# One scan and one product for both channel halves in the selective scan of a hybrid network

## The reference

```python
dt = softplus(dt_lo @ dt_proj_w.T + dt_proj_b)
A = -exp(A_log)
def step(h, inp):
    dt_t, B_t, C_t, x_t = inp
    dA = exp(dt_t[..., None] * A[None])
    h = dA * h + dt_t[..., None] * B_t[:, None, :] * x_t[..., None]
    return h, sum(h * C_t[:, None, :], axis=-1)
_, ys = lax.scan(step, h0, (dt, Bp, Cp, xc))
y = (moveaxis(ys, 0, 1) + Dp * xc) * silu(z)
return einsum('bti,di->btd', y, out_proj_w)
```

## Time and profile before

| what | value |
|---|---|
| median of three runs | 5252.44 us |
| the profiled execution | 5253.41 us |
| its span in the trace | 5251.6 us |
| mean granted TensorE clock | 0.91 |
| share of the span, PE / DVE / ACT / POOL | 80% / 65% / 54% / 38% |
| first and last scan instruction | 1345.4 us and 2366.6 us |

### The profile page before, as it was taken

The page is one execution under the profiler, slowest core; times in us unless marked ns, Lnnn a source line. Parts: engine busy times, 40 slices in busy tenths (PEclk is TensorE's granted clock), DMA queues, the critical chain, the costliest instruction groups (busy, mean ns, idle before and its releaser), DMA issues. The chain is left out here.

```text
span 5251.6 us, 108370 instructions
## 1 busy us (share of the span) xinstructions
PE 4205.7 (80%) x31331; PEld 2104.6 (40%) x31332; DVE 3399.0 (65%) x8427; ACT 2852.9 (54%) x5677; POOL 1970.2 (38%) x2539
## 2 busy tenths in 40 slices
PE   6499999899576766779868888886987788878698
PEld 3144444452222222226312222225973333333597
DVE  3488888448799899894478777762116766665212
ACT  7255555666555555557747676672324455555232
POOL 3000000011677777770403433344536144444452
PEclk9699999999899899899979899897999888888799
DMA  7522222005100000000532222224656332332466
GB/s 259 140 74 73 73 73 74 23 0 197 65 26 26 26 26 26 26 26 0 203 90 81 70 77 72 70 62 133 212 173 224 92 84 79 83 84 62 143 213 191
DMA packets 530984, 489.50 MB, mean 93 GB/s; under 512 B 160546, under 2 KB 468067, under 8 KB 530560
## 3 DMA queue, kind: packets, MB, share of 16 engines
q1 hardware_dynamic: 512496, 448.21, 28.7%
q0 software_dynamic: 18160, 37.42, 2.0%
HBM read 324.32 MB, written 161.09 MB: 92 GB/s over the span
## 5 line engine op out<-in xcount | busy, mean ns | idle before, releaser
L1539 ACT ACTIVATE p_probs<-p_t_ps 128x512 f32<-128x512 f32 (+1 forms) x2304 | 1142.9, 551 | 778.4 <-PE p_t_ps L1353 230.8
L2122 PE MATMUL p_y_ps<-p_prod,c_ident 128*128 128x512 f32 x1024 | 555.8, 669 | 304.1 <-DVE p_prod L2307 299.2
L1366 PE MATMUL p_o_ps<-p_probs,p_v_st 128*32 128x256 f32 (+3 forms) x8704 | 775.8, 432 | 7.4 <-ACT p_o_sb L1525 7.0
L1335 PE MATMUL p_t_ps<-p_t_q,p_t_k 50*128 50x512 bf16 (+3 forms) x3072 | 540.9, 351 | 263.1 <-ACT p_probs L1539 154.8
L1603 DVE TENSOR_REDUCE p_row_max<-p_s_ps 128x1 f32<-128x512 f32 x1024 | 644.8, 681 | 150.4 <-PE p_s_ps L1304 116.0
L2256 POOL TENSOR_TENSOR p_dbx<-p_dtx,p_b_sb 128x512 f32<-128x512 f32 x512 | 632.8, 1272 | 120.6 <-ACT p_b_sb L2153 120.6
L2298 DVE TENSOR_TENSOR_SCAN p_state<-p_da,p_dbx 128x512 f32<-128x512 f32 x512 | 599.2, 1207 | 94.5 <-ACT p_da L2191 76.9
L1241 POOL TENSOR_TENSOR p_v_st<-p_v_raw,p_ones 128x128 f32<-128x128 f32 x192 | 87.5, 456 | 1414.1 <-PE p_o_ps L1366 1358.7
L1304 PE MATMUL p_s_ps<-p_s_k,p_s_q 48*128 48x512 bf16 (+3 forms) x3072 | 508.8, 356 | 122.6 <-DVE p_row_max L1600 49.1
L1600 DVE CUSTOM_DVE_ANT_0 p_tried<-p_s_ps,c_mask_row 128x512 bf16<-128x512 f32 (+3 forms) x1024 | 450.0, 486 | 218.1 <-PE p_s_ps L1304 159.6
L1600 DVE CUSTOM_DVE_ANT_0 p_tried<-p_s_ps,p_s_bias 128x512 bf16<-128x512 f32 (+3 forms) x1024 | 449.6, 485 | 133.8 <-PE p_s_ps L1304 131.3
(11 more groups left out here) (295 smaller groups left out, 7084.9 us busy)
## 6 DMA issues: line engine op xcount, KB each, us to landing
p_wb<-in_w SPq DMA_DIRECT2D x142, 512.0 KB
p_s_q<-stack_q SPq DMA_DIRECT2D x384, 96.0 KB
p_s_k<-stack_k SPq DMA_DIRECT2D x384, 96.0 KB
p_t_q<-stack_q SPq DMA_DIRECT2D x384, 96.0 KB
p_t_k<-stack_k SPq DMA_DIRECT2D x384, 96.0 KB
mamba_inputs<-p_out SPq DMA_DIRECT2D x17, 1536.0 KB, 5.7
p_inp<-mamba_inputs SPq DMA_DIRECT2D x17, 1536.0 KB
p_raw<-routed_rows SPq DMA_DIRECT2D x142, 130.0 KB
```

The costliest lines, as they stand in the source:

```text
L1335: mm = pe.matmul(out[r], t_k[rows, g % 2, pair, c * P:(c + 1) * P], t_q[rows, g % 2, pair, first:first + width], start=True, stop=not mask ...
L1366: mm = pe.matmul(o_ps[32 * j:32 * j + 32, at:to], v_st[:, g % 2, c, j, :], probs[:, g % 2, j, place[c] + at - first:place[c] + to - first] ...
L1539: act.activation(exps, tile, ACT.Exp, scale=scale).then_inc(expd, 1)
L2122: pe.matmul(y_ps[:, h], w["ident"], prod[:, k_slot(n, h, RS)], start=(n == 0), stop=(n == STATE - 1)).then_inc(acc_mm, 1)
```

## The change

Both halves lie side by side in slots of 2T = 1024 columns. One scan instruction runs over both; so that the second half starts at zero, the decay at column 512 is held at zero (set once, and ScalarE writes only 511 columns of the second half). One product with C reads the same 512 columns of C twice. The ring `dbx` has four slots of two halves (the same room), `state` and `prod` double and stay. The decay slots now take four PSUM banks, so C has one bank in place of two and the outgoing product uses B's bank. On VectorE the product of state n-1 stands behind the scan of state n, the gate in state 1. On ScalarE the decay of a state stands ahead of the copy of B, which goes two states ahead. GpSimd waits for a whole scan before it reuses a slot.

```diff
-    R = 8
+    R = 4
+    RP = 2
-    COPIED = 3
+    COPIED = 2
+    OUT_AT = 4
...
-        da = ph.ps("da", [P, RA, T])
-        b_ps, c_ps = ph.ps("b_ps", [P, T]), ph.ps("c_ps", [P, 2, T])
-        y_ps, out_ps = ph.ps("y_ps", [P, 2, T]), ph.ps("out_ps", [P, T])
+        da = ph.ps("da", [P, RA, 2 * T])
+        b_ps, c_ps = ph.ps("b_ps", [P, T]), ph.ps("c_ps", [P, T])
+        y_ps = ph.ps("y_ps", [P, 2, T])
+        out_ps = b_ps
...
-                pe.wait_ge(prod_ready, RS - 4 + 2 * (STATE * b + n) + 2)
-                pe.matmul(c_ps[:, n % 2], w["select"][:, STATE + n], bc[:, u], start=True, stop=True
+                pe.wait_ge(prod_ready, RS + STATE * b + n)
+                pe.matmul(c_ps[:, :], w["select"][:, STATE + n], bc[:, u], start=True, stop=True
...
+                pe.wait_ge(b_ready, 1 + (STATE * (b + 1) + OUT_AT + AHEAD + 1 if follows else STATE * (b + 1)))
...
+                    shared = n == OUT_AT + 1 and not first
+                    if not shared:
+                        next_b(b, u, n, last)
...
+                    sums(b, n, first)
+                    if shared:
+                        pe.wait_ge(added, b + 1)
+                        next_b(b, u, n, last)
...
+                    act.wait_ge(scanned, R + m - RA + 1)
+                    for h in range(2):
+                        if n == 0:
+                            act.wait_ge(dt_ready, 2 + 2 * b + h + 1)
+                        act.activation(da[:, n % RA, h * T + h:h * T + T], dt[:, u, h, h:T], ACT.Exp,
+                                       scale=rate[:, h, n:n + 1]).then_inc(da_ready, 1)
                     if n + COPIED < STATE:
                         copy_b(b, n + COPIED)
...
+                    pool.wait_ge(b_ready, 1 + m + 1)
+                    pool.wait_ge(scanned, m + 1)
...
+            dve.memset(da[:, :, T:T + 1], 0.0).then_inc(rate_ready, 1)
...
+                dve.tensor_tensor_scan(out=state[:, n % RS], data0=da[:, n % RA], data1=dbx[:, n % R], initial=0.0,
                                        op0=ALU.mult, op1=ALU.add).then_inc(scanned, 1)
...
+                dve.wait_ge(acc_mm, 2 * m + 2)
+                dve.tensor_tensor(prod[:, n % RP].rearrange("p (h t) -> p h t", h=2),
+                                  state[:, n % RS].rearrange("p (h t) -> p h t", h=2),
+                                  c_ps[:, :].unsqueeze(1).to_broadcast([P, 2, T]), ALU.mult).then_inc(prod_ready, 1)
...
-                    scan(b, n, 0)
-                    scan(b, n, 1)
-                    if n == 0 and not first:
+                    scan(b, n)
+                    if n:
+                        times_c(b, n - 1)
+                    elif not first:
+                        times_c(b - 1, STATE - 1)
+                    if n == 1 and not first:
                         gate(b - 1, 1 - u)
-                    times_c(b, n, 0)
-                    times_c(b, n, 1)
-                    if n == 6 and not first:
+                    if n == OUT_AT + 2 and not first:
                         add(b - 1)
```

More of the change, by code:

```diff
@@ L2052, in mamba_scan, with half @@
         block = ph.block()
-        def k_slot(n, h, ring=R):
-            return (2 * n + h) % ring
+        def half(h):
+            return slice(h * T, h * T + T)
         @block.sync
@@ L2105, in outward, with sums, next_b @@
                 mm.then_inc(out_mm, 1)
+            def sums(b, n, first):
+                m = STATE * b + n
+                pe.wait_ge(prod_ready, RS + m + 1)
+                for h in range(2):
+                    if n == 0 and not first:
+                        pe.wait_ge(gated_ready, 2 * b + h + 1)
+                    pe.matmul(y_ps[:, h], w["ident"], prod[:, n % RP, half(h)], start=(n == 0), stop=(n == STATE - 1)
+                              ).then_inc(acc_mm, 1)
+            def next_b(b, u, n, last):
+                if n + AHEAD < STATE:
+                    broadcast_b(b, u, n + AHEAD)
+                elif not last:
+                    broadcast_b(b + 1, 1 - u, n + AHEAD - STATE)
             def sequence(b, u, first=False, last=False):
                 for n in range(STATE):
[L2109 to L2112, removed]
+                    shared = n == OUT_AT + 1 and not first
+                    if not shared:
+                        next_b(b, u, n, last)
                     if n + 1 < STATE:
@@ L2126, in sequence @@
                         pe.matmul(y_ps[:, h], skip_w[:, h], inp[:, u, h], start=False, stop=False)
-                    if n == 4 and not first:
+                    if n == OUT_AT and not first:
                         outward(b - 1)
@@ L2141, in _ @@
             sequence(NB - 1, 1, last=True)
-            outward(NB - 1)
+            outward(NB - 1, follows=False)
         @block.scalar
@@ L2185, in sequence @@
                         copy_b(b + 1, n + COPIED - STATE)
[L2186 to L2192, removed]
                     if last:
@@ L2249, in sequence @@
                     m = STATE * b + n
+                    pool.wait_ge(b_ready, 1 + m + 1)
+                    pool.wait_ge(scanned, m + 1)
                     for h in range(2):
-                        k = 2 * m + h
-                        pool.wait_ge(b_ready, 1 + m + 1)
                         if n == 0:
                             pool.wait_ge(dtx_ready, 2 * b + h + 1)
-                        pool.wait_ge(scanned, k + 1)
-                        pool.tensor_tensor(dbx[:, k_slot(n, h)], dtx[:, u, h], b_sb[:, n % RB], ALU.mult
+                        pool.tensor_tensor(dbx[:, n % R, half(h)], dtx[:, u, h], b_sb[:, n % RB], ALU.mult
                                            ).then_inc(dbx_ready, 1)
```

43 lines of the change are left out of this document (16 added, 27 removed).

## The result

The changed kernel takes 5179.8 us in the median of four runs (5174.51 to 5186.83), the kernel before on the same chip 5251.77 (5236.01 to 5255.83). The ratio is 0.9869 [0.9846, 0.9893]: 1.3% faster, 72 us. The forecast was 40 us, so the direction was right and the gain was nearly twice as large.

The account below looks back on a forecast made before the run. VectorE was taken to set the pace, at 64.6 us a sequence. Per sequence 6.9 us gone and 3.9 added, taken as 2.8 less, gave 39 us over 14, with 1 more 40: 5212 against the median, range 5182 to 5243.

Parts of the forecast that it names:

- Merging: VectorE's paired scans and products become one each: 0.14 us saved a state, 3.43 to 3.29, 36 us over 256 states.
- R4: Rival: the merge does not pay, as two banks or repeated columns slow VectorE; 36 us back, 5248; chance 0.07.
- R3: Rival: each removed instruction's fixed part falls out whole, 83 ns more for each of 512, 5170; chance 0.03.
- The three waits: New VectorE waits per sequence: 0.85 before the addition, 1.5 before state 8's scan, 1.6 before the last scan.
- Dp and state 6: Old VectorE waits behind two Dp matmuls and the outgoing product go: 1.3 and 1.5 us a sequence.
- The loop's return: Every second sequence VectorE's own 2.13 us stays; most of the 1.18 behind it is covered, 0.5 a sequence gained.
- The clock: TensorE stretches at 1.2 GHz cost VectorE 1.0 us a sequence instead of about 2.4, so 1.4 gained.
- The spare time: Decays of state n+4 ready at 5.8 us, their scan due at 7.7: 1.7 us to spare on the chain.
- R2: Rival: less is lost, state 8's wait does not come or the clock costs nothing; 21 us, 5191; chance 0.12.
- the wait in state 8: VectorE waits 1.5 us before state 8's scan: late copy of B, two softplus parts, then the decays on ScalarE.
- R1: Rival: the chains are no looser at 1.2 GHz than before; 20 us come back, 5233; chance 0.22.
- R5: Rival: slower, new idle stretches lower TensorE's clock; at half the stage 78 us, 5290; chance 0.05.

Follow-up runs that it names:

- experiment 2: Changed kernel with its one scan and one product per state written as two each, one per half: 5017.95 us, 0.9909 of the kernel before.
- experiment 5: Changed kernel with step size in state 12 (0.9853), outgoing product behind state 8 (0.9829), both plus later addition (0.9788), then GpSimd's correction spread too (0.979).
- experiment 4: Changed kernel, VectorE's loop only: first run waits for its last product before the return, 4998.95 us (0.987); last run covers four sequences a turn, 4995.28 us (0.9878).
- experiment 1: Kernel before with only the new order; halves, two C banks and the outgoing product's own bank stay: 4971.92 us against 5066.54, 0.9814.
- experiment 3: Kernel before with the loop over sequences written out on VectorE alone: 5039.03 us, 0.9948; on GpSimd alone: 5059.17 us, 0.9997.

## Why the prediction came out too small

- **Merging.** Forecast 3.29 us a state, measured 3.31. The price by start-to-start distances was right: 0.12 saved instead of 0.14 (31 us instead of 36, experiment 2). Neither two banks nor repeated columns slow VectorE down (R4): 2283 and 1196 ns are less than twice 1207 and 669. And the fixed part does not fall out whole (R3): the 157 ns for a pair by the Trainium skill's formula (VectorE: DVE Perf Modes, The TRN2 errata) would be 80 us for all 512 instructions, and the runs give 31.
- **The three waits.** Forecast 0.85, 1.5 and 1.6; measured 0.72, 1.22 and 1.52, each in its place and with its releaser. Their causes hold: in experiment 5 the step size and the outgoing product were moved, and the 1.52 and the 1.22 went; the 0.72 went only with the later addition, which brought 1.41 elsewhere. Together they cost 0.5 us a sequence less than I counted (3.7 with their lost overlaps, for 4.2).
- **Dp and state 6.** Both gone, as forecast.
- **The loop's return: the first failed step.** I wrote that VectorE's own 2.13 stays and counted it at every second sequence, 1.05 each. It is 0. I took it for a fixed price of the return. It is a delay from the last issue, and what counts is how much work is queued in front of it. The new order queues a scan and a product (3.31 us) there, and the shorter body makes the delay itself smaller. Either alone takes most of it: with the long body 0.14 and 0.39 are left at the two returns of the last run of experiment 4, with nothing queued 0.8 in its first. I also counted it too often: the loop of six turns jumps back five times, not at each of seven pairs of sequences.
- **The clock: the second failed step.** "With 1.7 to spare I take 1.0; the ends are 0 and the old 2.4." It is 0: every sequence has the same 59.73 us, those with sums at 1.2 GHz too. Two things go into this, and no run parts them. The spare time (1.7 in the text, 1.9 by its own terms 7.7 and 5.8) was not used up; in experiment 1 it holds even sums of 3.78 us. And the slow stretches became shorter, while I had priced the cost by four passes of 3.78, which no longer occur. Part of the old price was also the return's (experiment 3).

The sum: states +0.3, waits -0.5, return -1.05, clock -1.0, together -2.25 us a sequence; the measured 59.73 lies 2.07 under the forecast of 61.8 (which rounds up the saving: the terms give 2.7, not 2.8). Times 14 this is 29 us, which with the 40 gives the 69 to 72 measured. Of the rivals, R2 with 5191 and R3 with 5170 lie about equally near. R2 is half right: the clock costs nothing, but the wait in state 8 did come, and it says nothing of the return. R3 is near by luck, since its cause fails in experiment 2. R1 needed the chains to be tight at 1.2 GHz, and they are loose; R5 needed the clock to fall, and it rose from 0.92 to 0.95.

What the change leaves behind is seen by setting experiments 1 and 2 side by side. The order alone gives 1.9%. Merging saves 1.9 us a sequence and with the shared bank brings waits of 3.7 us, of which 0.3 were there before. With the last waits moved (experiment 5), the merged form reaches 2.1% under the kernel before, the best of all that ran. That is 0.26% under the order alone, at the edge of what the intervals tell apart; the stages in the traces, 914.8 and 931.9, differ by 17 us.

## What to carry to other kernels

Put one independent step between a producer and its consumer on the bounding engine: here the work queued there covered the chains of the other engines, slow stretches of TensorE and most of the loop's return at once. Price a merge by start-to-start distances, and set against it every wait of a shared buffer and of an operand that must now be whole. When an instruction is moved to gain slack, look at what runs beside it in the new place; and before moving what a releaser label names, look at what else ended in the same 0.2 us.

## What was unexpected in the hardware

- A loop's return on VectorE shows as 2.1 us of idle time with a body of 508 entries and 45 instruction transfers in the stage, and as 0.74 with 254 entries and 10 transfers, although nothing was queued in front of that one (experiment 4).
- VectorE's step size, with two operands in SBUF, takes 684 ns beside an idle GpSimd and 1131 in the median, up to 2116, beside GpSimd's products.
- A wait with several semaphores can carry the wrong name: the 1.41 before the scan of state 12 says GpSimd, whose product for that state had ended 3.3 us earlier, and follows ScalarE's decay by 0.19 us.
